# Preparing batch 0's attention heads in two groups of ten, the first by VectorE, the second by GpSimd

## What is computed

```python
xn = layernorm(x)
s = attention(xn, Wq, Wk, Wv, Wo)       # 16 query heads, 4 key/value heads of 16 features
g = silu(gated_ffn(xn, w_gate_up, w_down))   # 1024 inner features
...
```

```python
q = (x @ Wq).reshape(b, s, 16, 16); k = (x @ Wk).reshape(b, s, 4, 16)
q, k = rope(q), rope(k)                  # rotates the first 8 features of each head
scores = q @ k.T / 4                     # softmax over 512 tokens follows, then @ v, @ Wo
```

## Time and profile before

| | us |
|---|---|
| median of 3 runs | 345.54 (345.4 to 347.27) |
| the profiled execution | 345.08 |
| its span on the core | 343.3 |
| PE busy | 315.3 |
| DVE busy | 228.9 |
| ACT busy | 158.7 |
| POOL busy | 61.5 |

### The profile page before, as it was taken

How to read it: one execution, slowest core, us unless ns; L and a number is a source line. 1 busy time by engine, 2 the same in 40 slices (tenths; PEclk the granted TensorE clock), 3 DMA queues, 4 the chain that set the end, 5 groups by cost and what they waited for, 6 DMA issues and landing times.

```text
span 343.3 us, 4810 instructions
## 1 busy us (share of the span) xinstructions
PE 315.3 (92%) x1602; PEld 186.8 (54%) x1602; DVE 228.9 (67%) x494; ACT 158.7 (46%) x289; POOL 61.5 (18%) x80
## 2 busy tenths in 40 slices
PE   2977989999999999999999999999989999999940
PEld 2645565454465454465545456556655676666630
DVE  3997848778475676877976763039898575446940
ACT  1476514575776655554474465523315622232310
POOL 5007750000010000000000002100503421033063
PEclk9999989999999999999999999999999999999995
DMA  7900019028091370400000006108934993038410
GB/s 250 406 6 2 0 49 201 1 61 191 1 207 45 83 169 1 124 0 3 1 1 3 0 1 207 41 2 326 361 95 118 392 428 140 30 124 258 165 53 20
DMA packets 19483, 39.19 MB, mean 114 GB/s; under 512 B 1826, under 2 KB 15363, under 8 KB 18176
## 3 DMA queue, kind: packets, MB, share of 16 engines
q1 hardware_dynamic: 17904, 35.69, 32.6%
q0 software_dynamic: 1552, 3.15, 2.6%
HBM read 34.54 MB, written 15.22 MB: 145 GB/s over the span
## 4 chain that ended last, share of the span: by engine, by line
PE 78%; DVE 15%; issue 3%; ACT 1%; DMA 1%; POOL 1%; DVEq 0%; POOLq 0%; ACTq 0%
PE ps L1728 12%; PE ps L1673 9%; PE ps L1641 8%; PE ps L1741 8%; PE ps L1663 7%; PE ps L1783 6%; PE ps L1799 6%; PE ps L1811 6%; PE ps L1546 3%; DVE nmax L1222 3%; PE ps L1580 2%; PE ps L1848 2%; PE ps L1525 2%; PE ps L1773 1%; DMA x<-in_x 1%
## 5 line engine op out<-in xcount | busy, mean ns | idle before, releaser
L1222 DVE TENSOR_REDUCE nmax<-ps 128x1 f32<-128x512 f32 x128 | 85.5, 687 | 35.0 <-PE ps L1641 34.3
L957 ACT ACTIVATE shared<-ps 128x512 f32<-128x512 f32 x128 | 74.1, 594 | 53.6 <-PE ps L1663 52.7
L1641 PE MATMUL ps<-experts 96*128 96x512 bf16 x128 | 48.2, 384 | 1.6 <-DVE experts L1229 1.1
L1663 PE MATMUL ps<-experts 99*128 99x512 bf16 x128 | 48.3, 382 | 0.0
L1741 PE MATMUL ps<-shared,experts 128*128 128x256 f32 x128 | 37.5, 386 | 0.0
L1673 PE MATMUL ps<-shared,experts 128*32 128x512 f32 x256 | 34.1, 605 | 0.3 <-ACT shared L957 0.3
L1641 PEld LDWEIGHTS ps<-experts 96*128 96x128 bf16 x128 | 12.5, 98 | 36.7 <-DVE nmax L1222 18.3
L1741 PEld LDWEIGHTS ps<-shared,experts 128*128 128x128 f32 x128 | 23.4, 190 | 8.9 <-issue 2.5
L965 ACT ACTIVATE experts<-ps 96x1024 bf16<-96x1024 bf16 x18 | 17.9, 1018 | 11.6 <-PE ps L1580 11.6
L1546 PE MATMUL ps<-late_weights,xnT 128*128 128x512 f32 (+1 forms) x64 | 22.5, 492 | 0.3 <-DVE shared L1134 0.3
L1783 PE MATMUL ps<-experts,shared 128*128 x88 | 20.9, 380 | 0.8 <-ACT shared L1032 0.8
(11 more groups left out here) (232 smaller groups left out, 516.9 us busy)
## 6 DMA issues: line engine op xcount, KB each, us to landing
experts<-in_experts SPq DMA_DIRECT2D x8, 1536.0 KB, 11.3
slot_rows<-in_empty SPq DMA_DIRECT2D x4, 2080.0 KB, 12.2
shared<-in_wgu SPq DMA_DIRECT2D x1, 2048.0 KB, 10.9
x<-in_x SPq DMA_DIRECT2D x2, 512.0 KB, 5.5
shared<-in_wdn SPq DMA_DIRECT2D x1, 1024.0 KB, 12.8
expert_results<-in_empty SPq DMA_DIRECT2D x1, 1024.0 KB, 6.9
token_rows<-x SPq DMA_DIRECT2D x1, 1024.0 KB, 16.0
token_rows<-gx SPq DMA_DIRECT2D x1, 1024.0 KB, 4.5
```

The lines of the kernel that those rows point to most:

```text
L957: nc.scalar.activation(probs[:, n % 2, hh, :], ps[:, 2 + hh % 2, :], ACT.Exp, scale=float(HD) ** -0.5).then_inc(s["exp_done"], 1)
L1222: nc.vector.tensor_reduce(nmax[:, 4 * t + hh:4 * t + hh + 1], ps[:, m % 2, :], AX, ALU.max, negate=True).then_inc(s["max_done"], 1)
L1641: nc.tensor.matmul(ps[:, m % 2, :], qs[0:KS, b, GR * g + hh, P * t:P * t + P], ks[0:KS, b, g, :], start=True, stop=True).then_inc(s["score ...
L1663: nc.tensor.matmul(ps[:, 2 + hh % 2, :], ks[0:KM, b, g, P * t:P * t + P], qs[0:KM, b, GR * g + hh, :], start=True, stop=True).then_inc(s[" ...
```

## The change

Batch 0's 20 heads become two groups of ten (GH = 10): eight query heads and two key heads each (GQ = 8). The host orders the weight columns by group, so that a group lies together. DVE prepares group 0 ahead of its plan, and subtracts the token rows' low parts behind this instead of ahead. POOL, which still waits for group 0's `parts_done` and does its two weight pieces first, prepares group 1 and then batch 1; its wait for `mparts_ready` is gone. ACT copies the projections of batch 0 by group, the second group behind the second token copies. PE projects three tiles of batch 1 ahead of the stacks and the fourth between scores 1 and 2 and after 2; gate 0 moves from ahead of the stacks into the score stage, which has eight fills instead of six. Five stacks of batch 0 (heads of group 0) stay there; the other five go to steps 0, 1, 1, 2 and 2, through bank 5. The ten stacks of batch 1 go to steps 5 to 10. Group 1's three slot copies are ACT's, in step 0; batch 1's stay DVE's, in step 5. Two weight pieces are rounded by ACT later than before. The stacks' PSUM banks are 4 to 7 instead of 4, 5, 2 and 3, with waits of the up and gate products to match. Cut to its core:

```diff
-STACK_ORDER = (8, 0, 1, 9, 2, 3, 4, 5, 6, 7)
+STACK_ORDER = (8, 0, 1, 2, 3, 9, 4, 5, 6, 7)
+FIRST_STACKS = 5
...
     for n, (to, of) in enumerate(((3, 0), (4, 0), (5, 1))):
-        due(0, n + 1, ("slots", to, of))
-    for c, where in enumerate(((1, 1), (2, 1), (3, 1), (4, 0), (5, 3), (6, 1), (7, 1), (8, 1), (9, 3), (10, 1))):
+        due(0, n, ("slots", 0, to, of))
+        due(5, n, ("slots", 1, to, of))
+    for c, where in zip(STACK_ORDER[FIRST_STACKS:], ((0, 3), (1, 1), (1, 3), (2, 0), (2, 2))):
+        due(*where, ("stack_T", 0, c))
+    for c, where in enumerate(((5, 3), (6, 1), (6, 3), (7, 2), (8, 1), (8, 3), (9, 2), (9, 3), (10, 1), (10, 3))):
         due(*where, ("stack_T", 1, c))
...
-    early(KD)
-    stacks = [("stack_T", 0, c) for c in STACK_ORDER]
-    plan += stacks[:3]
+    stacks = [("stack_T", 0, c) for c in STACK_ORDER[:FIRST_STACKS]]
+    plan += stacks[:3] + [("round_weights", 3)]
     later = []
     for m in range(16):
         plan.append(("score", m))
-        if m in (0, 1, 3, 4, 6, 7, 9):
-            plan.append(stacks[3 + (0, 1, 3, 4, 6, 7, 9).index(m)])
-        elif m in (5, 8, 10, 11, 12, 14):
+        if m in (1, 2):
+            plan.append(("proj", TB - 1, m - 1))
+        elif m in (3, 4):
+            plan.append(stacks[m])
+        elif m in (5, 6, 7, 8, 9, 11, 12, 14):
             if emit() == ("hidden", 0):
                 later.append(plan.pop())
+        if m == 2:
+            plan.append(("proj_out", 1))
...
             for stage in range(4):
-                if stage == 2:
-                    pool.wait_ge(s["mparts_ready"], 1)
-                prepare(1, stage, pool, nc.gpsimd, chain)
+                prepare(0, 1, stage, pool, nc.gpsimd, chain)
+            for stage in range(4):
+                prepare(1, None, stage, pool, nc.gpsimd, chain)
...
-            projections(0)
+            act.wait_ge(s["qkv_psum"], TB)
+            copy_group(0)
             for k in range(KD):
                 act.wait_ge(s["xnT_psum"], KD + k + 1)
                 nc.scalar.activation(xnT[:, k, S:2 * S], ps[:, KD + k, :], ACT.Copy).then_inc(s["xnT_ready"], 1)
-            round_weights(2)
-            round_weights(3)
-
+            copy_group(1)
+            copy_values(0, TB, TB)
             act.wait_ge(s["first_part"], 1)
             for to in (3, 4):
-                nc.scalar.activation(place_in_stack(to, 0, HEADS), place_in_stack(0, 0, HEADS), ACT.Copy).then_inc(s["slots_copied"], 1)
-            projections(1)
+                nc.scalar.activation(place_in_stack(to, 0, GQ, 0), place_in_stack(0, 0, GQ, 0), ACT.Copy).then_inc(s["slots_copied"], 1)
+            second_projections(0)
+            round_weights(2)
...
-            dve.wait_ge(s["qkv_psum"], TB)
-            for k in range(KD):
-                dve.wait_ge(s["x_high_ready"], k + 1)
-                nc.vector.tensor_tensor(x_low(0, k), xnT[:, k, 0:S], x_high(0, k).bitcast(F32), ALU.subtract).then_inc(s["x_low_ready"], 1)
...
             for stage in range(4):
-                prepare(0, stage, dve, nc.vector, chain)
-            nc.vector.tensor_copy(place_in_stack(5, 0, HEADS), place_in_stack(1, 0, HEADS)).then_inc(s["slots_copied"], 1)
+                prepare(0, 0, stage, dve, nc.vector, chain)
+            nc.vector.tensor_copy(place_in_stack(5, 0, GQ, 0), place_in_stack(1, 0, GQ, 0)).then_inc(s["slots_copied"], 1)
+            dve.wait_ge(s["qkv_psum"], TB)
+            for k in range(KD):
+                dve.wait_ge(s["x_high_ready"], k + 1)
+                nc.vector.tensor_tensor(x_low(0, k), xnT[:, k, 0:S], x_high(0, k).bitcast(F32), ALU.subtract).then_inc(s["x_low_ready"], 1)
...
+                    pe.wait_ge(s["xnT_ready"], B * KD)
+                    for t in range(TB - 1):
+                        for k in range(KD):
+                            projection(1, t, k)
...
+                    if m == 32:
+                        pe.wait_ge(s["misc_free"], misc_use[("stack_T", 0, STACK_ORDER[-1])] + 1)
...
-        "wqkv": deep(np.concatenate([a["L0_attn_Wq"], a["L0_attn_Wk"], a["L0_attn_Wv"]], axis=1)),
+        "wqkv": deep(np.concatenate([wq[:, :q_half], wk[:, :k_half], wq[:, q_half:], wk[:, k_half:], wv], axis=1)),
```

More of the change, by code:

```diff
@@ L28 @@
 QKH = HEADS + KVH
+GH = QKH // 2
+GQ = HEADS // 2
 INTER = 1024
@@ L601, in tiles_from, with place_in_stack @@
                 drain(i)
[L603 to L610, removed]
+        def place_in_stack(a, h0=0, h1=GH, group=None):
+            if group is None:
+                return stack.rearrange("p (r h) c -> p r h c", h=GH)[:, :, h0:h1, HD * a:HD * a + HD]
+            return stack.rearrange("p (j g h) c -> p j g h c", j=TB, h=GH)[:, :, group, h0:h1, HD * a:HD * a + HD]
@@ L611, in prepare @@
+        def prepare(b, group, stage, eng, ops, chain):
+            turn = b + 1 if b else group
+            n = QKH if b else GH
+            rows = qk[:, TB * b:TB * b + TB, 0 if b else GH * HD * group:QKH * HD if b else GH * HD * (group + 1)].rearrange("p j (h c) -> p j h c", c=HD)
             rot = rows[:, :, :, 0:8]
             pair = rot.rearrange("p j h (r two) -> p j h r two", two=2)
-            ta = rot_a[:, 0:TB * QKH * 8].rearrange("p (j h c) -> p j h c", j=TB, h=QKH)
-            tb = rot_a[:, TB * QKH * 8:TB * QKH * 16].rearrange("p (j h c) -> p j h c", j=TB, h=QKH)
+            ta = rot_a[:, 0:TB * n * 8].rearrange("p (j h c) -> p j h c", j=TB, h=n)
+            tb = rot_a[:, TB * n * 8:TB * n * 16].rearrange("p (j h c) -> p j h c", j=TB, h=n)
@@ L623, in prepare @@
+            high = stack.rearrange("p (j h) c -> p j h c", j=TB)[:, :, :, 0:HD] if b else slot(0)
             if stage == 0:
-                eng.wait_ge(s["qk_copied"], 2 * (b + 1))
-                if b:
-                    eng.wait_ge(s["parts_done"], b)
+                eng.wait_ge(s["qk_copied"], 2 * B if b else group + 1)
+                if turn:
+                    eng.wait_ge(s["parts_done"], turn)
                     eng.wait_ge(s["const_loaded"], 16)
-                ops.tensor_tensor(ta, rot, angle("cos0", 8, [P, TB, QKH, 8]), ALU.mult)
+                ops.tensor_tensor(ta, rot, angle("cos0", 8, [P, TB, n, 8]), ALU.mult)
@@ L942, in _ @@
                     qkv1_out(it[1])
+                elif kind == "round_weights":
+                    round_weights(it[1])
+                elif kind == "proj_out":
+                    second_projections(it[1])
+                elif kind == "slots" and it[1] == 0:
+                    to, of = it[2:]
+                    act.wait_ge(s["parts_in" if of else "first_part"], 2)
+                    nc.scalar.activation(place_in_stack(to, 0, GQ, 1), place_in_stack(of, 0, GQ, 1), ACT.Copy).then_inc(s["slots_copied"], 1)
                 elif kind == "raw_T":
@@ L1490, in _, with projection @@
             pe.wait_ge(s["const_loaded"], 16)
+            def projection(b, t, k):
+                j = TB * b + t
+                last = nc.tensor.matmul(ps[:, 4 - 4 * b + t, 0:384], xnT[:, k, P * j:P * j + P], wqkv[:, k, :],
+                                        start=k == 0, stop=k == KD - 1)
+                if k == KD - 1:
+                    last.then_inc(s["qkv_psum"], 1)
             keep_warm(WARM_UP, 7)
@@ L1579, in _ @@
                             at_ = (a * TB + t) * P
-                            last = nc.tensor.transpose(src[:, at_:at_ + P], stack[:, QKH * t + 2 * c + a, :], identb[:])
+                            last = nc.tensor.transpose(src[:, at_:at_ + P], stack[:, QKH * t + row_in_stack + a, :], identb[:])
                     last.then_inc(s["stack_T"], 1)
@@ L1626, in _ @@
                     last.then_inc(s["logits"], 1)
+                elif kind == "proj":
+                    projection(1, *it[1:])
                 elif kind == "score":
```

106 lines of the change are left out of this document (57 added, 49 removed).

## The result

The change makes the kernel slower: 352.05 us in the median of four runs (351.43 to 352.66) against 345.47 for the kernel before beside it, a ratio of 1.020 with an interval of 1.017 to 1.024. The forecast was 343.9, with a range up to 346.5. The profiled execution took 352.44 us, with a span of 350.4 against 343.3.

The account below looks back on a forecast made before the run. PE, busy 92% of the span and all the time from 53 us, sets the end; ahead, DVE's preparation bounds. 4.1 - 2.25 + 0.15 - 0.35 = 1.65 us gained, giving 343.9 us, 8-in-10 range 341.9 to 346.5.

Parts of the forecast that it names:

- DVE's first group: Head of the program: preparing ten heads on DVE takes 4.35 us plus 0.21 for the slot copy, done about 23.3.
- PE and ACT ahead of the first stack: Head of the program: first stack at 23.75 against 28.03, first score at 26.4, 4.28 us earlier.
- the score stage: PE's scores and fills with DVE's row maxima: the maxima end at 38.8 against 42.91, 4.1 us earlier.
- the paragraph on POOL: POOL's preparation: group 1 done at 37.5, over 18 us to spare; batch 1's parts at 77, wanted about 81.
- Rival (b): Ahead of the first score, POOL's weight subtraction holds DVE's moved token-row subtraction, up to 2.4 us; 346.3 us, chance 0.10.
- The moved stacks: Steps 0 to 2, where PE is saturated: five batch-0 stacks at 0.45 each, 2.25 us lost.
- The batch-1 slot copies go to step 5: 0: Step 5, where DVE is busy 27.31 of 42.0: moving batch 1's slot copies there costs nothing.
- ACT's crowding: Steps 1, 2, 6, 8, 9 and 10, with two ACT stack copies each: 0.35 us lost, between 0 and 5.8.
- ACT over 90% in steps 1 and 2: Sign that the forecast is right: ACT some 10.3 us busy in 11.35, 91%, with three more copies.
- Rival (d): ACT becomes the bound in six steps with paired stack copies, 5.8 us lost; 349.3 us, chance 0.09.
- rival (a): Around PE's 2.24 us stand: the clock drop is averted or stacks sink into waits, up to 2 us more; 342.0, chance 0.20.

Follow-up runs that it names:

- e1: Changed kernel plus two POOL waits for mparts_ready: ahead of batch 1's rotation (first unit's) and of its cast (second unit's); 346.63 us, ratio 1.0064.
- e5: e1 with batch 1's slot copies in step 4 instead of 5 and its ten stacks placed so the last comes earlier; 344.63 us, ratio 0.9999.
- e8: Kernel before, with POOL summing two unused SBUF tiles of 1024 columns where it would only wait; run once, 344.68 us.
- e3: Changed kernel plus only a POOL wait for the first unit's mparts_ready ahead of batch 1's rotation; 350.56 us, ratio 1.0177.
- e7: Kernel before, with POOL filling two unused tiles of 1024 columns with zeros where it would only wait; run once, 345.21 us.
- e2: Changed kernel plus only a POOL wait for the second unit's mparts_ready ahead of batch 1's cast; 348.59 us, ratio 1.0124.
- e9: Changed kernel without added waits, batch 1's cast and subtraction on POOL cut into four instructions each; 348.92 us, ratio 1.0094.
- e4: Kernel before, without POOL's wait for mparts_ready ahead of stage 2, nothing else changed; 348.04 us, ratio 1.0113.
- e6: e1 without its second wait, three group-1 stacks in PE's stand, two in step 0, batch 1's slot copies and stacks from step 3; 341.90 us, ratio 0.9939.
- e10: e6 without POOL's remaining wait for mparts_ready, so batch 1's rotation runs beside the first unit's max_parts again; 343.54 us, ratio 0.9971.

## Why the prediction was wrong, point by point

**DVE's first group, PE and ACT ahead of the first stack, the score stage: right.** 4.32 us earlier at the last maximum, forecast 4.1. The half-sized instructions cost what was read from the pairs of sizes (the rotation's 0.48, 0.32, 0.32, 0.49, casts 0.49).

**The step that failed** is the sentence behind the score stage: "The delayed product, the 2.24 us wait and what follows up to the first probabilities are issued in the same order with the same number of fills done (16 before as after): a shift, no change." The order was the same, but DVE's four small instructions have a partner on another engine, and POOL had moved under them. In the paragraph on POOL I asked only who waits for POOL (group 1 was done at 37.2, forecast 37.5; batch 1's cast began at 69.9, forecast 66, and nobody waited for it), not whom POOL would hold while it ran, and I gave the removed wait for `mparts_ready` no price at all. Yet it stood in my own rows: the 1.79 us of idle time ahead of POOL's L639, released by DVE's L1259. At 38.5 and at 70 us POOL was where `max_parts` is. By the ratios the two collisions, with the clock behind them, cost 4.8 us (`e1` against the changed kernel).

**Rival (b) had the mechanism at the wrong place.** I weighed the lock for the token rows' subtraction. There DVE came first (23.35 to 24.63), and POOL's L786, started at 24.28, took 2.58 us, where the same weight piece took 2.40 before: POOL was held a little, if at all, and nobody waited. Nor was DVE held in its stack copies out of PSUM. I should have gone through all of DVE's instructions between 24 and 75 us that have two SBUF inputs or a fast mode, not only the one that the change moved. Its chance of 0.10 and price of 2.4 us were too small for that.

**The moved stacks**: five for 2.25 us. No run has this alone; on PE's timeline each takes its 0.45 us (59.27 to 59.72 for the first), and `e5`'s account above has room for them. That the price was right doesn't show that nothing else was lost with them: one of the five was late for its score by 0.68 us.

**"The batch-1 slot copies go to step 5: 0"** was wrong by 0.79 us. They cost DVE nothing, but PE waits for the third of them at the first stack, and DVE takes it behind its row maxima. The date of a copy's user counts, not the load of its engine.

**ACT's crowding**, 0.35 taken: PE's waits for ACT are 1.1 us in `e1`, both at the last stack of a batch and its user, not in the steps with paired copies as such. The sign "ACT over 90% in steps 1 and 2" did not come either: ACT is busy 4.74 of 6.30 us in step 1 (75%) and 7.97 of 10.0 from 62 to 72 us, where 91% had been reckoned. Rival (d), ACT as the bound, did not happen; rival (a) neither: the clock fell further.

For the profiled executions the terms add up so: -4.3 head, +1.0 first collision, +1.4 clock behind it, +2.2 second collision (PE's stand; DVE itself loses 3.0, 3.70 us instead of 0.70), +1.3 clock behind it (values 2 to 3, against `e1`), +2.25 stacks, +0.8 and +1.1 waits: 5.8 of the 6.7 us at step 11. The 0.9 left over I can't assign; about as much is missing in the same account of `e5` (0.7).

## What to carry to other kernels

When work moves onto GpSimd or in time on it, list what VectorE does at that time: its casts and its two-input instructions in SBUF may each be held for the rest of a GpSimd instruction, even those of 16 columns, and on a critical chain a 0.17 us instruction became one of 2.48 us here. A wait that keeps the two apart, shorter GpSimd instructions, or another date for the work were each worth more here than the time that they cost GpSimd. And before a wait on an idle engine is removed, ask what it kept apart; before work is moved behind a saturated stretch, look for a stand of that engine which can take it.

## What the runs showed that was not expected

The clock's loss does not follow from the length of one stand. In the score stage's stand PE's granted clock stayed at 1.00 in `e8` (3.20 us) and in `e1` (2.23 us), and fell to about 0.8 for some microseconds in the kernel before, `e3` and `e5` (2.23 or 2.24 us), in `e7` (2.84 us) and in the changed kernel, `e2` and `e9` (3.20 to 3.24 us); in `e4` (4.75 us) it was 0.60. In `e6` and `e10`, whose waits there are 1.03 us at most, it stayed at 1.00. So between 2.2 and 3.2 us these traces show no dependence on the length, only that it mostly falls; that short waits avoid it rests on two traces.

Nor does it need a stand: behind the router products it fell in `e1`, `e3`, `e9` and `e10` and not in the other profiled executions, for some 1.5 us each time (19.7 or 19.8 us from values 20 to values 23 against 18.3). Since one kernel's executions differ in this, medians that lie 1 to 2 us apart need the trace beside them. The 19 executions of the kernel before beside `e5` reach from 343.39 us, at a mean clock of 0.989, to 348.44 us, at 0.972. In `e8` its one execution took 344.68 us, no longer than the kernel before, though its first small instruction was held for a microsecond.
